# An attention and mixture-of-experts layer on one core: the experts' first product turned from fp32 into three fp32r terms

## The reference, cut to what matters

```python
x = layernorm(x + attention(x))          # x: 4 x 1024 x 512, 16 heads of 32
x = layernorm(x + ffn(x))

def ffn(x):                              # 4096 tokens of 512, 8 experts, 2 for each token, all in float32
    scores = xf @ gate_w.T
    ew, ei = top_k(scores, 2); ew = softmax(ew)
    x1 = silu(einsum('td,ehd->teh', xf, w_gate))      # each expert: 512 -> 256
    x3 = einsum('td,ehd->teh', xf, w_up)
    expert_out = einsum('teh,edh->ted', x1 * x3, w_down)
    routed = (expert_out weighted by ew, summed over a token's two experts)
    shared = silu(xf @ sh_gate.T) * (xf @ sh_up.T) @ sh_down.T   # 512 -> 512 -> 512
    return routed + sigmoid(xf @ se_gate_w.T) * shared
```

## Time and profile before

| what | us |
|---|---|
| time of three runs: median | 2083.41 |
| lowest and highest | 2080.54, 2083.98 |
| the profiled execution, by the same clock as those runs | 2082.21 |
| its span in the trace, first to last instruction | 2080.5 |
| TensorE busy | 2013.2 (97%) |
| VectorE busy | 1277.8 (61%) |
| ScalarE busy | 879.3 (42%) |
| GpSimd busy | 867.7 (42%) |

### The profile page before, as it was taken

How to read it: one execution, slowest core, us unless ns; L and a number is a source line. 1 busy time by engine, 2 the same in 40 slices (tenths; PEclk the granted TensorE clock), 3 DMA queues, 4 the chain that set the end, 5 groups by cost and what they waited for, 6 DMA issues and landing times.

```text
span 2080.5 us, 30213 instructions
## 1 busy us (share of the span) xinstructions
PE 2013.2 (97%) x9764; PEld 1222.7 (59%) x9765; DVE 1277.8 (61%) x2281; ACT 879.3 (42%) x1563; POOL 867.7 (42%) x829
## 2 busy tenths in 40 slices
PE   7999999999999999999999988999999999999997
PEld 5655555655556655556655435688444444446886
DVE  5877776677776677775677856573222222225875
ACT  2266654466664466664366674311111111112332
POOL 3255654455654455654455557200111111114651
PEclk9999999999999999999999999999999999999999
DMA  7312434312334322434321325822222222225762
GB/s 232 72 41 68 97 78 102 127 46 64 98 77 103 127 53 56 98 79 102 126 51 38 73 73 204 315 78 71 92 90 91 91 85 86 91 76 168 227 177 72
DMA packets 95922, 213.00 MB, mean 102 GB/s; under 512 B 24304, under 2 KB 24816, under 8 KB 92592
## 3 DMA queue, kind: packets, MB, share of 16 engines
q1 hardware_dynamic: 84992, 175.96, 28.7%
q0 software_dynamic: 10800, 35.40, 6.3%
HBM read 118.51 MB, written 41.93 MB: 77 GB/s over the span
## 4 chain that ended last, share of the span: by engine, by line
PE 84%; SPq 4%; DMA 3%; DVE 3%; issue 2%; POOL 2%; ACT 1%; another core or an unknown queue 1%; ACTq 0%; POOLq 0%; DVEq 0%
PE ps_gu L1684 12%; PE ps_s L724 11%; PE ps_side L702 11%; PE ps_ctx L735 10%; PE ps_side L676 8%; PE ps_gu L1622 8%; PE ps_d L1707 6%; PE ps_sum L748 5%; PE ps_d L1622 4%; SPq L359 3%; DMA inv_rows<-inv_few 2%; PE ps_t L1674 1%; PE pr_s L1254 1%; PE ps_hts L1697 1%; PE ps_side L724 1%
## 5 line engine op out<-in xcount | busy, mean ns | idle before, releaser
L999 DVE TENSOR_REDUCE max_half<-ps_side 128x1 f32<-128x512 f32 x1024 | 658.6, 682 | 202.4 <-PE ps_side L702 199.3
L702 PE MATMUL ps_side<-kq_stack 96*128 96x512 f32 x1024 | 408.9, 404 | 4.9 <-DVE max_half L999 2.3
L724 PE MATMUL ps_s<-kq_stack 97*128 97x512 f32 x937 | 392.4, 420 | 7.8 <-ACT probs_first L888 4.8
L724 PEld LDWEIGHTS ps_s<-kq_stack 97*128 97x128 f32 x937 | 177.5, 190 | 165.4 <-issue 85.5
L1578 POOL DMA_INDIRECT x_g<-x,who_all x71 | 67.3, 948 | 471.3 <-PE ps_t L1674 355.5
L1684 PE MATMUL ps_gu<-gu_sb,xT_e 128*128 x568 | 258.6, 598 | 0.8 <-issue 0.6
L888 ACT ACTIVATE probs_first<-ps_s 128x512 f32<-128x512 f32 x326 | 187.5, 600 | 106.6 <-PE ps_s L724 90.8
L702 PEld LDWEIGHTS ps_side<-kq_stack 96*128 96x128 f32 x1024 | 195.1, 191 | 57.3 <-DVE max_half L999 26.3
L888 ACT ACTIVATE probs_mid<-ps_s 128x512 f32<-128x512 f32 x308 | 177.5, 599 | 111.7 <-PE ps_s L724 97.1
L623 POOL TENSOR_TENSOR acc<-probs_first,probs_mid 128x512 f32<-128x512 f32 x129 | 163.8, 1297 | 132.2 <-ACT probs_mid L888 132.2
L888 ACT ACTIVATE probs_last<-ps_s 128x512 f32<-128x512 f32 x303 | 175.5, 599 | 98.6 <-PE ps_s L724 82.3
(11 more groups left out here) (238 smaller groups left out, 3303.2 us busy)
## 6 DMA issues: line engine op xcount, KB each, us to landing
kq_stack<-kq SPq DMA_DIRECT2D x192, 256.0 KB, 5.1
y_slots<-y_t SPq DMA_DIRECT2D x71, 256.0 KB, 2.3
x_r<-x SPq DMA_DIRECT2D x32, 256.0 KB, 3.8
x_t<-x SPq DMA_DIRECT2D x32, 256.0 KB
gu_sb<-wgu SPq DMA_DIRECT2D x8, 1024.0 KB, 15.2
out<-gu_sb SPq DMA_DIRECT2D x32, 256.0 KB, 2.6
res<-inv_rows SPq DMA_DIRECT2D x124, 64.0 KB, 2.0
stage<-wkqT SPq DMA_DIRECT2D x28, 256.0 KB, 3.1
```

What stands on the lines that cost most here:

```text
L702: nc.tensor.matmul(bank, q_stack[par][0:3 * HD, h, t * P:(t + 1) * P], k_stack[par][0:3 * HD, h, half * HALF:(half + 1) * HALF], start=Tru ...
L724: nc.tensor.matmul(out, k_stack[par][0:3 * HD + 1, h, kt * P:(kt + 1) * P], q_stack[par][0:3 * HD + 1, h, half * HALF:(half + 1) * HALF], ...
L999: nc.vector.reduce_max(max_half[:, u // 2, u % 2:u % 2 + 1], bank, AX.X).then_inc(side_free, 1)
```

## The change

- Experts' first product: in place of four fp32 products for a tile, twelve fp32r products in the three terms of the shared layers (`three`), with weights `gu_hi` and `gu_lo`. The gathered tile is split too: ScalarE's copy now writes the high part (`xT_hi`), and VectorE has a new operation in each expert step, `expert_x_low`, between the product of gate and up and the copy of y. TensorE waits for it (`et_low`).
- Low weights: GpSimd makes them in place, over `gu_sb`, in 32 pieces of 128x512: a copy to fp32r (`gu_part`, two buffers) and a subtraction. It starts when all of `gu_sb` has landed and the scores are done, and its gathers of x come behind all 32.
- High weights: the pieces in `gu_part` are stored to memory (`gu_kept`) by SP behind the base stores of steps 2 to 8. The shared weights (`sgu_hi`, `sgu_lo`, `sd_hi`, `sd_lo`, 6 MB) are stored to memory behind step 3. When TensorE has used the gate and up weights for the twelfth tile, SP loads the experts' high weights (8 MB, two loads of 1 MB in flight) to where the shared weights lay and into four small buffers behind them. The first four expert tiles wait for their expert's weights, the loop for all.
- At the end of the experts SP loads the shared weights back: `sgu_hi` behind store 67, the others when the last first product is done, ahead of the last store of y. For tile 12 TensorE computes all terms with `sgu_hi` first, then waits for `sgu_lo`.
- SP's order: the loads of the shared up and down weights stand behind the tiles 15 and 19 of the scores, not ahead of tile 12. All `gu_sb` loads come ahead of the `wd_sb` loads.
- The order of buffers in SBUF changes, and two unused parts (a semaphore, `e_xT`) go.

```diff
@@ attention, SP's tail
-                for k in range(1, 3):
-                    load_shared(k)
                 for t in range(12, TT):
...
                     load_r(t)
+                    if t in (15, 19):
+                        load_shared(1 if t == 15 else 2)
@@
+KEEP_AFTER = 3
+PARTS_STORED_AFTER = {2: range(0, 4), 3: range(4, 9), 4: range(9, 14), 5: range(14, 19), 6: range(19, 24),
+                      7: range(24, 29), 8: range(29, 32)}
@@ feed_forward, SP
+            def store_part(i):
+                sp.wait_ge(router.st_high, 3 * C + i + 1)
+                sp.dma_start(gu_kept[i // C, :, i % C, :], gu_part[:, i % 2, :].bitcast(F32)).then_inc(part_out[i % 2], 16)
+
+            def load_high(e):
+                sp.dma_start(gu_hi[:, e].bitcast(F32), gu_kept[e]).then_inc(hi_in[e % 2], 16)
+
+            def high_landed(e):
+                sp.wait_ge(hi_in[e % 2], 16 * (e // 2 + 1))
+                sp.sem_inc(hi_known, 1)
@@
-                sp.dma_start(wd_sb[:, e], wd[e]).then_inc(gu_in, 16)
-            for t in range(COVER):
+            for e in range(E):
+                sp.dma_start(wd_sb[:, e], wd[e]).then_inc(wd_in, 16)
+            for t in range(COVER - 2):
                 store_base(t)
                 load_tile(t + 4)
+                for i in PARTS_STORED_AFTER.get(t, ()):
+                    store_part(i)
+                if t == KEEP_AFTER:
+                    for part, to in zip((sgu_hi, sgu_lo, sd_hi, sd_lo), shared_at):
+                        sp.dma_start(to, part[:].bitcast(F32)).then_inc(shared_kept, 16)
+            for i in range(2):
+                sp.wait_ge(part_out[i], 16 * (E * C // 2))
+            sp.wait_ge(router.st_split, 3 * C + E * C)
+            sp.wait_ge(shared_kept, 16 * 4)
+            sp.wait_ge(gu_ready, COVER)
+            sp.sem_inc(passed, 1)
+            load_high(0)
+            load_high(1)
+            store_base(COVER - 2)
+            load_tile(COVER + 2)
+            for e in range(2):
+                high_landed(e)
+                load_high(e + 2)
+            store_base(COVER - 1)
+            load_tile(COVER + 3)
+            sp.wait_ge(d_ready, COVER)
...
+            sp.wait_ge(eh_ready, 2 * TOKENS // P)
+            sp.dma_start(sgu_hi[:].bitcast(F32), shared_at[0]).then_inc(router.st_in[0], 16)
             for t in range(NT // 4 * 4, NT):
+                if t == NT - 1:
+                    sp.wait_ge(eh_ready, NT)
+                    sp.dma_start(sgu_lo[:].bitcast(F32), shared_at[1]).then_inc(router.st_in[1], 16)
+                    for part, at in ((sd_hi, shared_at[2]), (sd_lo, shared_at[3])):
+                        sp.dma_start(part[:].bitcast(F32), at).then_inc(router.st_in[2], 16)
                 store_slots(t, t % 4)
@@ feed_forward, GpSimd
+            pool.wait_ge(gu_in, 16 * E)
+            pool.wait_ge(router.sc_ready, TT // 4)
+            pool.sem_inc(passed, 1)
+            for i in range(E * C):
+                e, c = i // C, i % C
+                if i >= 2:
+                    pool.wait_ge(part_out[i % 2], 16 * (i // 2))
+                nc.gpsimd.tensor_copy(gu_part[:, i % 2, :], gu_sb[:, e, c, :]).then_inc(router.st_high, 1)
+                pool.wait_ge(router.st_high, 3 * C + i + 1)
+                nc.gpsimd.tensor_tensor(gu_lo[:, e, c, :], gu_sb[:, e, c, :], gu_part[:, i % 2, :].bitcast(F32),
+                                        ALU.subtract).then_inc(router.st_split, 1)
             pool.wait_ge(who_known, 1)
@@ feed_forward, TensorE
+            def up_high_first(t):
+
+                pe.wait_ge(router.st_in[0], 32)
+                for k in range(2):
+                    for c in range(C):
+                        for x in (xT_hi, xT_lo):
+                            nc.tensor.matmul(ps_gu[:, k, :], x[:, t % 2, c, :], sgu_hi[:, c, k, :],
+                                             start=c == 0 and x is xT_hi, stop=False)
+                pe.wait_ge(router.st_in[1], 32)
...
@@ expert_up
                 pe.wait_ge(et_done, t + 1)
+                pe.wait_ge(et_low, t + 1)
+                if static(t, 4):
+                    pe.wait_ge(hi_known, e + 1)
...
-                    done = nc.tensor.matmul(ps_gu[:, s % 2, :], e_xT[:, s % 2, c, :],
-                                            gu_sb[:, bass.ds(e, 1), c, :].rearrange("p a n -> p (a n)"),
-                                            start=c == 0, stop=c == C - 1)
+                    high, low = [w[:, bass.ds(e, 1), c, :].rearrange("p a n -> p (a n)") for w in (gu_hi, gu_lo)]
+                    done = three(ps_gu[:, s % 2, :], (xT_hi[:, s % 2, c, :], xT_lo[:, s % 2, c, :]), (high, low), c, C - 1)
@@ feed_forward, VectorE
+            def expert_x_low(t, s):
+                dve.wait_ge(et_done, t + 1)
+                if not static(t, 2):
+                    dve.wait_ge(eh_ready, t - 1)
+                nc.vector.tensor_tensor(xT_lo[:, s % 2], ps_t[:, s % 2, :].rearrange("p (c t) -> p c t", c=C),
+                                        xT_hi[:, s % 2].bitcast(F32), ALU.subtract).then_inc(et_low, 1)
@@ expert_step
                 expert_hidden(t, s)
+                if not is_last(t):
+                    expert_x_low(t + 1, (s + 1) % 4)
@@ build
-            gu_sb = sb("gu_sb", [P, E, C, 2 * H])
+            with nc.sbuf_tensor("gu_sb", [P, E, C, 2 * H], F32) as gu_sb:
+                pass
+            gu_lo = sb("gu_lo", [P, E, C, 2 * H], F32R)
             wd_sb = sb("wd_sb", [P, E, CH, D])
+            with nc.sbuf_tensor("gu_hi", [P, E, C, 2 * H], F32R) as gu_hi:
+                pass
```

More of the change, by code:

```diff
@@ L1425, in feed_forward @@
         ps_who, ps_count = ps_hts[:, 1, 0:NT], ps_hts[:, 1, P:2 * P]
-        x_in = [sem(f"xt_in{i}") for i in range(4)]
+        x_in = router.x_in
+        x_before = TT // 4
         t_ready = sem("t_ready")
@@ L1480, in turns_of, with expert_pipeline @@
             return 4 * (t - s)
-        def expert_pipeline(eng, step):
+        def expert_pipeline(eng, step, between=None):
             step(0, 0)
@@ L1485, in expert_pipeline @@
                 step(s, s)
+            if between is not None:
+                between()
             with eng.Fori(1, NT // 4) as j:
@@ L2075, in _ @@
             finish(COVER - 1)
+            expert_x_low(0, 0)
             expert_pipeline(dve, expert_step)
```

75 lines of the change are left out of this document (50 added, 25 removed).

## The result

The changed kernel takes 2055.18 us (median of four runs, 2050.72 to 2056.95) beside 2083.05 us of the kernel before (2080.54 to 2083.98): a ratio of 0.9864, 95% interval 0.9849 to 0.9878, so 28 us faster, where I had said 44. That lies in the wide range of 2025 to 2060 us, which takes in three of the rivals, but 6 us above the forecast's own range of 2027 to 2049; the point is 16 us off, and the rival "the lock in full" with 2053.7 us came nearest. The profiled execution took 2056.95 us, its span is 2055.2 us, and its granted clock (the share of TensorE's full clock of 2.4 GHz that it was given) was 0.988 in the mean.

What follows compares the result with a forecast made beforehand. TensorE was taken to bound the kernel, busy nearly all the time. From 2082.2 us, -49.7 + 3.3 - 6.2 + 6 + 3.3 = -43.3 gave 2039 us; own range 2027 to 2049, wide range 2025 to 2060.

Steps and rivals of the forecast that it cites:

- three of the rivals: Table operations all waiting for GpSimd (2053.7 us, 18%), late high weights (2049 us, 8%), late low half (2050 us, 6%).
- the lock in full: Rival in the cover: each VectorE table operation waits for one of GpSimd's, 20.7 us instead of 6, total 2053.7 us; 18%.
- Experts' product, -49.7 and +3.3 for register work: Expert tiles: twelve fp32r products replace four fp32, 0.70 us less for each of 71; added register operations cost 3.3 us.
- VectorE's low half "hidden with 0.4 us to spare": Expert loop: VectorE's extra 0.69 us operation ends at T + 2.0, before TensorE asks at T + 2.38; T ends the first product.
- Hidden by 3 us: 0: Entry to the experts: all eight high-weight loads known by 1476 to 1478, tile 4 asks at 1481; cost 0, at most 10 us.
- the stop ahead of tile 0: Entry: a stop of TensorE ahead of expert tile 0 or 4 was listed as a sign that the forecast is wrong.
- the rival that I had priced at 10 us and 8%: Rival at the entry: high weights come late and TensorE stands before tile 4, 10 us, total 2049 us; 8%.
- Scores, -6.2: Scores: moving two 1 MB loads behind tiles 15 and 19 removes 3.85 us idle and the slow work behind it, 6.2 us.
- I see no wait in its place: Scores: the moved 1 MB loads, 2.5 us each, would cause no new TensorE wait for x tiles.
- Tables, +6: Cover, steps 3 to 6: VectorE's table operations delayed by GpSimd's splitting cost 6 us, between 1 to 2 and 20.7.
- Exit, +3.3: End of the experts: 1.7 us from waiting for reloaded low weights and 1.6 us for hidden(13); bounds 0 and 10.

Runs made afterwards that it cites:

- best_two: Changed kernel with reordered entry and exit, two tables in step 3 while GpSimd idles, one each in steps 4 to 9, 6 MB stored behind step 1: 2034.91 us.
- after_again: The changed kernel run once more, unaltered, on the chip of the other kernels of its group: ratio 0.9868 to the kernel before.
- all_three: Changed kernel with tables spread over steps 3 to 8, first low half ahead of finish(11), four high-weight loads in flight, low weights reloaded earlier: 2044.83 us.
- split_between: Changed kernel, but GpSimd makes nine pieces before VectorE's first table, then splits only when a step's tables are made: 2054.11 us.
- entry_exit: Changed kernel with first low half ahead of finish(11), four high-weight loads in flight, low gate and up weights fetched ahead of last store but one: 2046.68 us.
- tables_spread: Changed kernel with VectorE's eight tables spread over steps 3 to 8 instead of two in each of steps 3 to 6: 2049.69 us.

## Why the prediction was right and wrong

The forecast had the direction and the wide range right and its middle wrong. The table stage held what its own rival described, and three of the terms that came out right did so partly by luck.

- **Experts' product, -49.7 and +3.3 for register work: -46.4, measured -45.8** (-47.7 in best_two). The mechanism is right: twelve products take 2.76 us and not 2.74, which makes 48.3 us and not 49.7. The register work is mis-sized: I put once more 0.05 us a tile for it, and it adds nothing, since the loop's turns cost 16 times 0.37 us in both kernels. That the sum still agrees to 0.6 us is luck: a slow first product (1.8 us) and the wait at tile 1 (0.8) stand in for it.
- **VectorE's low half "hidden with 0.4 us to spare": right** in the steady state, wrong at the entry, where I costed nothing and looked at the weights only. "Hidden by 3 us: 0" failed in two ways: `finish(11)` ahead of the low half cost 1.8 us of waiting, the stop ahead of tile 0 that I had named as a sign of being wrong (and 1.8 of a slow first product in this execution, though not in after_again); and the eight loads take not 24 us but about 31 until they are used (in all_three from 1465.2 to TensorE's start of tile 4 at 1496.2), so that tile 4 waited 1.8 to 4.9 us in five of the profiles, though not in this kernel's first: the rival that I had priced at 10 us and 8%.
- **Scores, -6.2: mis-sized**, -3.9 here and -4.5 alone. The slow clock went as I had said. "I see no wait in its place" was wrong: x tiles are still waited for, 1.40 and 0.75 us of idle time here where the kernel before has 0.67 beside its 3.85.
- **Tables, +6: the step that failed.** The idle time is 6.0 us, the very term, but by luck, since it is no case of mine: the eight small comparisons do wait for GpSimd, and where they do two tables take 11.5 to 13.5 us for 5.9. They cost 2.2 us behind step 3 and 3.8 behind step 6; behind step 4 they cost nothing because TensorE was late itself, and in step 5 GpSimd stood behind the 6 MB of stores, as I had said. What was not in the sum is what TensorE does behind such a wait: 10.7 us lost at half clock. I had this in hand: the earlier trace rows show 3.85 us of idle time and 2.4 us of slow work behind it, and I used them for the wait that goes, but not for the waits that come.
- **The lock in full, 20.7 us, 18%**: its mechanism, the small comparisons waiting too, holds; its price came near (+18.7) for another reason, since 6.0 of it are waiting and the rest is clock. The Trainium skill, SBUF — State Buffer, section "Who interferes with whom", says which operations of VectorE contend with GpSimd: copies, casts and tensor_scalar operations from SBUF to SBUF in the modes that use both pairs of ports, and those with two SBUF inputs, but not those with at most one SBUF input outside these modes. The trace agrees for the comparisons from SBUF to SBUF (304 to 1293 ns), for an operation of two SBUF operands (0.42 us in the kernel before, 1.38 in split_between), and for the low half and hidden, which read one operand from PSUM and stay at 0.67 to 0.69 us beside a busy GpSimd.
- **Exit, +3.3: measured +3.7, partly by luck.** The wait for the low weights is as I had it (2.3 us for 2). But I had 1.6 us of waiting for hidden(13) as new, and the kernel before already stood 2.4 us at that place; what is new there is 1.4 us of slow clock behind the wait, again the price that I had left out. The gather and the combine come 2 us later than I had them.

So 12.7 of the 18 us missed are in the cover, 2.3 in the scores, 2.0 at the entry; the remainder is a microsecond.

What stays open: why the clock fell behind some gaps and not behind others of the same length. And all_three's exit is 4.7 us shorter: 1.6 us are the shorter wait for the low weights, and its wait for hidden(13) and the slow clock behind it are gone (its first combine comes at T + 19.2), but exits of kernels that don't differ there spread by some 2 us.

## What to carry to other kernels

Price a wait of TensorE twice: the idle time, and what runs at half clock behind it. In the changed kernel's cover that was 1.6 to 2.2 times the wait again, but it does not grow with the wait: by the granted clock, some 3.4 to 6.4 us were lost behind waits of 2.0 to 5.5 us in these runs, and 1.7 behind the one of 9.85. And don't add such prices up over neighbouring steps: an engine that is late does not wait for the next hand-over. Work that a second engine takes over beside a full critical engine is free only where it does not stretch a chain that the critical engine waits for; look for what stands *queued ahead* of that hand-over on the engine between them, and count its time with the neighbour busy. And where contention can't be removed, spread its victims: best_two has the same slow comparisons and pays nothing for them.

## What the runs showed of the hardware

- VectorE's comparison of 128x71 in fp32 from SBUF took 304 ns alone and up to 1293 ns beside GpSimd's copies and subtractions of 128x512; GpSimd's own 0.61 us copy went up to 1.61, its 1.28 us subtraction up to 2.24 (2.34 in best_two). Both sides lose.
- Idle times of TensorE of 2.0 to 9.9 us ahead of the turn of hidden in the cover were followed within 2 us by a granted clock of 0.50 (1.2 GHz), in all 13 places where the profiles of these runs have one; with 2.7 us of unused products in the wait, and 0.39 us left of it, the clock stayed at 1.00. Waits of 1.0 to 1.7 us there left it up.
- Elsewhere the length of the wait did not decide. Ahead of expert tile 4 the clock fell behind 1.83, 2.55 and 4.85 us of idle time, and stayed at 1.00 behind 2.75 (all_three) and 3.00 (entry_exit). At the wait for the low weights it stayed behind 2.19 and 2.28 us and fell behind 2.33, 2.46 and 2.66. The same gap of 1.84 us at the entry was followed by a slow first product in the changed kernel and in tables_spread, and not in after_again.
